# Local attention in six layers: the mask as eight small products, keys transposed before the output product, and three moved steps on VectorE and ScalarE

## What is computed

```python
for i in range(DEPTH):                                   # DEPTH = 6
    x = attn_layer(shift_tokens(x), Wqkv[i], q_scale[i], k_scale[i], Wo[i]) + x
    x = ffn_layer(shift_tokens(x), ...) + x

def attn_layer(x, Wqkv, qs, ksc, Wo):                    # 16 heads of 64
    q, k, v = jnp.split(x @ Wqkv, 3, -1)                 # by head
    q = l2norm(q) * qs; k = l2norm(k) * ksc
    q = q * cos * scale + rotate_half(q) * sin * scale
    k = k * cos * inv + rotate_half(k) * sin * inv
    out = local_attention(q, k, v)                       # windows of 32 queries
    return out @ Wo

# local_attention: a window of 32 queries looks at its own 32 keys and the 32 before
mask = (it < jb) | (it > jb + w) | (jb == -1)
sim = jnp.einsum('bhwie,bhwje->bhwij', bq, bk2) * QK_SCALE
sim = jnp.where(mask, -jnp.finfo(sim.dtype).max, sim)
out = jnp.einsum('bhwij,bhwje->bhwie', softmax(sim), bv2)
```

## Time and profile before

| | |
|---|---|
| median of 3 runs | 5129.18 us (5128.84 to 5138.17) |
| profiled execution, device time | 5126.68 us |
| its span in the trace | 5124.9 us |
| TensorE busy | 4668.2 us, 91% |
| VectorE busy | 3785.3 us, 74% |
| ScalarE busy | 2776.0 us, 54% |
| GpSimd busy | 2074.7 us, 40% |
| granted TensorE clock, mean | 0.968 of 2.4 GHz |

### The profile page before, as it was taken

The page is one execution under the profiler, slowest core; times in us unless marked ns, Lnnn a source line. Parts: engine busy times, 40 slices in busy tenths (PEclk is TensorE's granted clock), DMA queues, the critical chain, the costliest instruction groups (busy, mean ns, idle before and its releaser), DMA issues. The chain is left out here.

```text
span 5124.9 us, 167765 instructions
## 1 busy us (share of the span) xinstructions
PE 4668.2 (91%) x74640; PEld 2826.5 (55%) x74640; DVE 3785.3 (74%) x4462; ACT 2776.0 (54%) x3791; POOL 2074.7 (40%) x1499
## 2 busy tenths in 40 slices
PE   7858987998789869999999999999999999999998
PEld 5623334444333346665666466655666566746664
DVE  5667883333778568886888588868887688868885
ACT  4527774223467645555555455555555455555554
POOL 4330000001000046654666366636665466546661
PEclk9979998999799989999999999999999999999999
DMA  0021111000111121111111111111111111111110
GB/s 23 12 69 32 44 43 34 1 0 27 59 38 43 28 62 40 40 37 45 40 40 40 43 40 40 39 40 40 40 40 52 31 40 40 36 43 40 40 40 26
DMA packets 95777, 192.82 MB, mean 38 GB/s; under 512 B 27088, under 2 KB 45520, under 8 KB 93264
## 3 DMA queue, kind: packets, MB, share of 16 engines
q1 hardware_dynamic: 95056, 182.09, 13.9%
HBM read 60.36 MB, written 15.73 MB: 15 GB/s over the span
## 5 line engine op out<-in xcount | busy, mean ns | idle before, releaser
L1846 POOL TENSOR_TENSOR part_of_layer<-part_of_layer,sine_of_layer 128x512 f32<-128x512 f32 x768 | 963.1, 1275 | 640.0 <-DVE sine_of_layer L1718 640.0
L1853 POOL TENSOR_TENSOR part_of_layer<-part_of_layer,inverse_of_layer 128x1024 f32<-128x1024 f32 x384 | 730.3, 1902 | 325.0 <-ACT inverse_of_layer L1601 310.0
L967 ACT ACTIVATE prob_of_ca<-ps 128x1024 f32<-128x1024 f32 (+3 forms) x768 | 594.0, 814 | 263.5 <-PE ps L841 197.6
L1715 DVE TENSOR_TENSOR part_of_layer<-ps,rope 128x1024 f32<-128x1024 f32 x384 | 467.6, 1218 | 46.8 <-ACT square_of_layer L1589 36.0
L1632 ACT ACTIVATE values_of_layer<-ps 128x1024 f32<-128x1024 f32 x192 | 196.5, 1024 | 516.3 <-PE ps L1488 516.3
L1718 DVE TENSOR_TENSOR sine_of_layer<-ps,rope 128x1024 f32<-128x1024 f32 x384 | 465.1, 1211 | 0.0
L859 PE MATMUL ps<-keys_of_ca,queries_of_ca 64*128 64x512 bf16 (+3 forms) x1536 | 331.1, 342 | 133.7 <-DVE top_of_ca L999 60.9
L1507 PEld LDWEIGHTS ps<-prob_t_of_layer,mixed_of_layer 64*64 64x64 f32 x12288 | 338.0, 134 | 161.0 <-issue 151.7
L1416 PE MATMUL ps<-qkv,shifted 128*128 128x512 f32 x768 | 384.3, 622 | 26.8 <-POOL values_of_layer L1856 20.4
L1758 DVE TENSOR_REDUCE total_of_layer<-prob_of_layer 128x16 f32<-128x1024 f32 x192 | 234.2, 1220 | 229.1 <-ACT prob_of_layer L1625 229.1
L1507 PE MATMUL ps<-prob_t_of_layer,mixed_of_layer 64*64 64x32 f32 x12288 | 385.6, 220 | 10.6 <-ACT prob_t_of_layer L1616 6.7
(11 more groups left out here) (206 smaller groups left out, 9248.5 us busy)
## 6 DMA issues: line engine op xcount, KB each, us to landing
mixed_of_layer<-values_of_layer SPq DMA_DIRECT2D x636, 128.0 KB
mixed_of_layer<-values_of_layer SPq DMA_DIRECT2D x264, 64.0 KB
queries_of_ca<-q_parts SPq DMA_DIRECT2D x384, 32.0 KB
keys_of_ca<-k_parts SPq DMA_DIRECT2D x384, 32.0 KB
qkv<-in_qkv SPq DMA_DIRECT2D x6, 1536.0 KB, 6.5
q_parts<-parts_of_ci SPq DMA_DIRECT2D x16, 384.0 KB, 2.6
k_parts<-parts_of_ci SPq DMA_DIRECT2D x16, 384.0 KB, 2.6
rope<-in_rope SPq DMA_DIRECT2D x6, 1024.0 KB, 9.0
```

Source lines behind the costliest of these rows:

```text
L967: nc.scalar.activation(prob[:, i % 2, 2 * two:2 * two + 2, j:], ps[:, 2 * two:2 * two + 2, j:], ACT.Exp, scale=scale).then_inc(raised, 1)
L1715: nc.vector.tensor_tensor(part[:, t % 2, side], by_head(slot), table(2 * side, t), ALU.mult).then_inc(parts, 1)
L1846: nc.gpsimd.tensor_tensor(out, out, sine[:, side, :, (1 - to) * half:(2 - to) * half], ALU.add).then_inc(rotated, 1)
L1853: nc.gpsimd.tensor_tensor(part[:, t % 2, side], part[:, t % 2, side], by, ALU.mult).then_inc(scaled, 1)
```

## The change

On TensorE the mask is added by eight products of a 32x32 identity with 32 rows of the table (four windows of 32 queries times two halves of the heads) instead of two products of a 128x128 identity with all 128 rows. The table for the first tile of a sequence now masks the look-back in every window's rows, and only window 0 of that tile uses it. `turn_k` stands behind `turn_q`, ahead of `project`. On VectorE `even` stands behind the query rotation of the next step, and `lengths` is cut in two: the keys' sums stand behind `shift`. The lower bound is now a second instruction of each half, and `invert` on ScalarE is cut in two as well, the keys' half behind `raise_p`.

```diff
                 def score(t):
                     reach(pe, l, k_out, t + 1)
-                    for h in range(2):
-                        nc.tensor.matmul(two_banks(SCORE_SLOT)[:, h, :], k["ident_b"][:, :],
-                                         w["band"][:, int(t % TILES == 0), :], start=True, stop=False)
+                    for i in range(P // WIN):
+                        for h in range(2):
+                            rows = slice(h * WIN, (h + 1) * WIN)
+                            nc.tensor.matmul(two_banks(SCORE_SLOT)[i * WIN:(i + 1) * WIN, h, :], k["ident_b"][rows, rows],
+                                             w["band"][rows, int(t % TILES == 0 and i == 0), :], start=True, stop=False)
...
-                    steps((make_next_q, 0), (make_k, 0), (turn_q, 1), (project, 3), (last(lambda: turn(1)), 2), (turn_k, 1),
+                    steps((make_next_q, 0), (make_k, 0), (turn_q, 1), (turn_k, 1), (project, 3), (last(lambda: turn(1)), 2),
                           (turn_p, 2), (score, 1), (last(lambda: turn(0)), 1), (make_v, 0), (weigh, 2),
...
-                def invert(t):
+                def invert(t, side, guarded, logged, inverted):
+                    at = slice(side * HEADS, (side + 1) * HEADS)
                     reach(act, l, guarded, t + 1)
-                    nc.scalar.activation(root[:, t % 2], length[:, t % 2], ACT.Ln).then_inc(logged, 1)
+                    nc.scalar.activation(root[:, t % 2, at], length[:, t % 2, at], ACT.Ln).then_inc(logged, 1)
                     reach(act, l, logged, t + 1)
-                    nc.scalar.activation(inverse[:, t % 2], root[:, t % 2], ACT.Exp, scale=-0.5).then_inc(inverted, 1)
+                    nc.scalar.activation(inverse[:, t % 2, at], root[:, t % 2, at], ACT.Exp, scale=-0.5).then_inc(inverted, 1)
...
-                    steps((square_next_q, 0), (square_k, 0), (out_q, 1), (out_k, 1), (out_p, 2), (last(first_invert), 2), (invert, 0),
-                          (out_v, 0), (raise_p, 1), (last(lambda: square_of(0)), 1), (out_o, 2), (shift_low, 4))
+                    steps((square_next_q, 0), (square_k, 0), (out_q, 1), (out_k, 1), (out_p, 2), (last(first_invert), 2), (invert_q, 0),
+                          (out_v, 0), (raise_p, 1), (last(lambda: square_of(0)), 1), (invert_k, 0), (out_o, 2), (shift_low, 4))
...
-                def lengths(t):
-                    reach(dve, l, q_squared, t + 1)
-                    nc.vector.reduce_sum(length[:, t % 2, 0:HEADS], square[:, 0], AX_X).then_inc(summed, 1)
-                    reach(dve, l, k_squared, t + 1)
-                    nc.vector.reduce_sum(length[:, t % 2, HEADS:], square[:, 1], AX_X).then_inc(summed, 1)
+                def lengths(t, side, squared, guarded):
+                    mine = length[:, t % 2, side * HEADS:(side + 1) * HEADS]
+                    reach(dve, l, squared, t + 1)
+                    nc.vector.reduce_sum(mine, square[:, side], AX_X).then_inc(summed, 1)
+                    reach(dve, l, summed, 2 * t + side + 1)
+                    nc.vector.tensor_scalar(mine, mine, LEAST_SQUARE, None, ALU.max).then_inc(guarded, 1)
...
-                    steps((rotate_q, 0), (lengths, 0), (guard, 0), (rotate_k, 0), (maxima, 1), (shift, 1), (last(first_centre), 1),
-                          (add, 3), (totals, 1), (even, 1), (last(second_centre), 1), (last(third_centre), 2))
+                    steps((rotate_q, 0), (even, 2), (lengths_q, 0), (rotate_k, 0), (maxima, 1), (shift, 1), (last(first_centre), 1), (lengths_k, 0),
+                          (add, 3), (totals, 1), (last(second_centre), 1), (last(third_centre), 2))
...
-    band = np.stack([seen, seen & ((at >= WIN)[:, None] | (key >= 0)[None, :])], 1)
+    band = np.stack([seen, seen & (key >= 0)[None, :]], 1)
```

23 lines of the change are left out of this document (15 added, 8 removed).

## The result

| | median, us | ratio to before, 95% interval |
|---|---|---|
| before | 5132.97 (5128.84 to 5138.17, 4 runs) | |
| changed | 5295.35 (5292.32 to 5307.08, 4 runs) | 1.0325 (1.0313 to 1.0337) |

The change makes the kernel 162 us slower; 5262 had been predicted, with 5200 to 5325 as the range. The profiled execution of the changed kernel took 5307.08 us, with a span of 5305.3.

A forecast was written before the change was run, and what follows sets the result against it. TensorE's own program was taken to bound each step. Per layer 28 x 0.61 = 17.1, plus 2.6, minus 2.1, plus 4.7 = 22.3 us, 134 in six layers, gave 5262 us, range 5200 to 5325.

The forecast's parts named there:

- The wait: Keys' transposes cannot start before 5.57, behind the chain product, squares, two rotation products; TensorE waits 1.16 each step.
- The step: Undisturbed step: 14.17 + 1.16 - 0.41 = 14.92, less 0.14 gained at the mask: 14.78, 0.61 more.
- the best bound: Mask: all eight products at once, 0.32 from mask to scores, gain 0.22 instead of 0.14.
- The poor end of the range: Mask with 0.10 more for the extra tiling switch, head 0, tail +6: 28.5 a layer, 5300.
- The split sums: VectorE, ScalarE: first part hidden; second lower bound ends near 15.25, copy starts 0.99 after the step; `shift_low` costs 2.6 a layer.
- The head: Steps 1 to 3 of a layer: rotation comes earlier with `even` behind it; -2.1 us, between 0 and -3.
- The tail: Layer's end: last `even` behind `second_centre` 3.7 later, output product behind keys' transposes adds 1.0; +4.7, between +3 and +6.
- Mask pieces two or one at a time: Mask's products run two at a time, 5359, chance 0.08; or wholly serial, 5507, chance 0.03.
- ScalarE late in each step: Second lower bound held by GpSimd's addition, ScalarE's copy ends past the squares' place: 101 us more, 5363, chance 0.06.
- Faster, by stretches of TensorE's own that the wait absorbs: Stretches before the new wait absorbed, mask's 0.54 gone too, tail free: 5121; chance 0.03, 0.01 for over 0.2% faster.
- A wrong reading of the code: Keys' transposes would start at 4.41, without waiting for VectorE; given no chance of its own.
- The clock in the steps: New wait drops TensorE's clock, a fifth of steps at 1.2 GHz: about 400 us more, 5662, chance 0.03.

The follow-up runs named there:

- keys_only: The kernel before with only the keys' transposes moved ahead of the output product: 5285.54 us, ratio 1.0305.
- cut2: The kernel before with the keys' transposes placed after two of the output product's eight parts: 5205.86 us, ratio 1.0149.
- cut6: The kernel before with the keys' transposes placed after six of the output product's eight parts: 5090.72 us, ratio 0.9921.
- mask_only: The kernel before with only the mask's eight products and the new table: 5115.12 us, ratio 0.9971.
- last_even_back: The changed kernel with `even` of each layer's last tile put back behind `totals`: 5253.35 us, ratio 1.0242.
- even_only: The kernel before with only `even` moved behind the next step's query rotation: 5190.7 us, ratio 1.0118.
- keys_back: The changed kernel with the keys' transposes put back behind the output product: 5236.1 us, ratio 1.0206.
- after_cut6: The changed kernel with the last tile's `even` put back and the keys' transposes after six of the output product's eight parts: 5206.74 us, ratio 1.0147.
- split_only: The kernel before with only sums, lower bounds and inverse norms split by queries and keys: 5136.13 us, ratio 1.0014.

## Why the prediction was right, and where its terms were off

**The wait: right.** It was put at 5.57 after the step's start; measured 3450.66 - 3445.08 = 5.58. It carries the verdict: keys_only costs 3.05%, and cut2 and cut6 follow the same number. That nothing shortens the chain held against the kernel before, where the rotation starts at 3.08 as it does now. But with the transposes moved and `even` left in its place the rotation would usually have been at 3.29 (keys_only). So the moved `even` keeps some 0.2 a step from being lost, which the prediction did not see: its 14.92 for the step before the mask's gain is 15.15 in keys_only's median.

**The step: 14.78 predicted; measured 14.84 at the shortest, 14.92 in the median.** Most of the difference to the shortest is the mask, taken as 0.40 from mask to scores. It is 0.34 (3454.32 to 3454.66), near the best bound, that of all eight at once. But the time from the probabilities' transposes to the mask grew as well. keys_only has the old mask with no wait before it (timeline):

```profile
2704.11 1.04 PE L1459 MATMUL ps<-sb_ident,prob_of_layer 128*128 128x128 f32 x8
2704.99 0.59 PE L1466 MATMUL ps<-band,sb_ident_b 128*128 128x512 bf16 x2
2705.51 1.49 PE L1475 MATMUL ps<-keys_of_layer,queries_of_layer 64*32 64x64 f32 x128
```

Here 0.88 and 0.52, in the changed kernel 0.97 and 0.34. The gain is 1.40 - 1.31 = 0.09, not 0.14. The extra 0.09 stands just where the array goes from whole to 32x32 pieces. The Trainium skill (TensorEngine Tiling (Array Packing), Key Properties) says that a change of tiling mode drains TensorE. The trace agrees so far as it has 0.09 more in that place. The poor end of the range held 0.10 for it, the sum nothing. In mask_only the 0.09 lies under the wait for ScalarE's copy, so the mask earns the full 0.20 there.

**The split sums: right in their end, wrong in the reading of the first half.** Second lower bound until 15.25: measured 4384.95 + 0.48 - 4370.00 = 15.43. Copy of the weighted values 0.99 after the step: 0.81 (4370.81). `shift_low` pushes by 0.2 (squares at 2.23 instead of 2.03), not 0.43, so 1.2 a layer for 2.6. The first lower bound was to be hidden; it is 1.23 long, since I left out what `even` does to GpSimd. What stood behind the sum, "the new wait absorbs", was true and covered this too. The Trainium skill (SBUF — State Buffer, SBUF: two separate sides) names this case: a VectorE instruction with two inputs in SBUF and a GpSimd instruction that reads SBUF exclude each other for a whole instruction. `even` is such a one and the rotation, whose one input is in PSUM, is not; the trace agrees with 3.42 and 3.35 beside `even`, 2.52 without.

**The head: -2.1 predicted, about -0.7 measured** (38.4 us from step 0 to step 3, before 39.1).

**The tail: +4.7 predicted, +9.5 measured.** This is the term with the largest error, 4.8 x 6 = 29 of the 33 us missing. Its mechanism was right: the last `even` waits behind `second_centre`. Its size was worked out at full clock.

The experiments split it. The order on TensorE alone is worth 2.2 (keys_only, 109.1) and is what is left without the late `even` (last_even_back, 2.0 over before); for it 1.0 had been taken. The late `even` is worth 7.5 (last_even_back) to 7.9 (even_only); for it 3.7 had been taken, its own delay and nothing behind it. The end of the third layer's attention, TensorE in the changed kernel (timeline; before: the earlier trace rows):

```profile
3462.96 1.39 PE L1450 MATMUL ps<-sb_ident,part_of_layer 128*128 128x128 f32 x8 [1.92 <-POOL part_of_layer L1867]
3464.14 3.33 PE L1522 MATMUL ps<-heads_out_of_layer,wo 128*128 128x128 f32 x16
...
3475.56 3.78 PE L1522 MATMUL ps<-heads_out_of_layer,wo 128*128 128x128 f32 x16 [2.19 <-ACT heads_out_of_layer L1632]
...
3483.63 1.57 PE L1461 MATMUL ps<-sb_ident,prob_of_layer 128*128 128x128 f32 x8 [3.43 <-DVE prob_of_layer L1780]
...
3491.09 3.58 PE L1522 MATMUL ps<-heads_out_of_layer,wo 128*128 128x128 f32 x16
```

and the granted clock of the first 40 us of it (busy times by engine, clock, DMA share), with the same stretch of the kernel before in the second fence:

```profile
3459.46:3500.00 40.54, 30.02 (x539) 25.66 (x533) 17.71 (x28) 15.39 (x24) 6.46 (x6) 0.75 0.17 52
```

```profile
3371.26:3408.00 36.74, 30.33 (x528) 23.22 (x522) 21.97 (x33) 18.08 (x27) 7.45 (x7) 0.95 0.30 104
```

The output product, 1.95 at full clock, takes 3.33, 3.78 and 3.58: it runs at 1.2 GHz for most of that time (granted clock 0.56, 0.50 and 0.52). In this layer even the first of them does, and so the mask behind it stands 3.8 later than before, counted from the last step's start (3468.27 - 3445.08 = 23.19, before 3376.57 - 3357.15 = 19.42). In three of the six layers (the first, fourth and fifth) that product is still at full clock, and the mask is about 2 later. The last probabilities are transposed 38.55 after the last step's start instead of 30.85, so `even` adds 3.9 here, near the 3.7 predicted. What the prediction lacked comes behind: from there to the last output product it is 2.1 longer, and that product itself 1.5. Before, only one output product of the three in this layer fell to that clock. The idle times ahead of the slow ones (1.92, 2.19, 3.43 here, 1.35 before) are longer.

The same end in last_even_back (timeline of TensorE) has its last output product at full clock:

```profile
3457.89 2.05 PE L1522 MATMUL ps<-heads_out_of_layer,wo 128*128 128x128 f32 x16 [0.56 <-ACT heads_out_of_layer L1632]
```

So it is in all six layers of last_even_back and in five of before. In the changed kernel and in even_only this product is slow in all six. The lower clock at the end thus comes with the late `even`.

**The rivals.** Mask pieces two or one at a time: no, 0.34. ScalarE late in each step: not in the changed kernel, but it is what keys_back and after_cut6 show, by another route than I wrote. Faster, by stretches of TensorE's own that the wait absorbs: hardly, the time over the shortest step is 29, some 7 of it `shift_low`'s, before 25. A wrong reading of the code: no, the transposes waited. The clock in the steps: no, 1.01 of idle time in 14.85 left it at 1.00 (stretch 3023.74 to 3430.00):

```profile
3023.74:3430.00 406.26, 379.32 (x8641) 264.19 (x8642) 369.50 (x379) 237.00 (x331) 265.01 (x169) 1.00 0.16 38
```

**The sum** by measured terms: 28 x 0.70 (mean steps 15.01 against 14.31, `shift_low` in them) = 19.6 where 19.7 had been predicted, head -0.7, tail +9.5: 28.4 a layer, 170 in six. The two profiled executions differ by 5307.1 - 5126.7 = 180, since that of the changed kernel is the longest of its runs; the medians differ by 162. Of the 10 us between 170 and 180, 6.4 lie ahead of the first layer, in code that the change does not touch (its first queries' product starts at 1833.3, before at 1826.9), and 3 at the last layer's end, which is 12.4 longer and not 9.5 (137.1 against 124.7 from the last step to the end).

That 19.6 meets 19.7 is luck in part. The shortest step is 0.68 longer and not 0.61, 2.0 more a layer; the push by `shift_low` is 1.4 less, and TensorE's own stretches take 0.6 less than before.

## What to carry to other kernels

When a group is moved on the engine that bounds the kernel, work out the earliest time at which what it waits for can be there, and the place it would get; the same move gains up to that point and loses from it on, and a part of the covering work (here six of eight pairs) can be left in front. An edit tested alone says little about a kernel with another edit in it: a long wait on the bounding engine hides what the helpers do, and where it is taken away their own ring comes out. Where a stage drains at its end, price what stands there at the lower clock.

## What the runs showed that was not expected

- Eight bf16 products on 32x32 pieces with 512 columns each take 0.34 from the first to the scores, where two whole ones take 0.52. Ahead of them, where the array goes from whole to 32x32 pieces, stand 0.09 more.
- `even` on VectorE (inputs in SBUF) holds GpSimd's additions by 0.9, and a lower bound on 16 numbers a partition waits up to 1.23 for them.
- The same holds the other way round: where `even` comes while GpSimd's product with the inverse norm is running, it takes 1.70 to 1.98 (medians of keys_only and split_only; 1.33 before).
- TensorE has holes of about 1.1, mostly in the weighting, with no semaphore behind them. All 167 of 0.6 us and more end 1.18 to 1.61 us after a 16 KiB packet of the instruction queue. The time over the shortest step went 25, 42, 82 us for 0, 6 and 14 more instructions a step, and 113 where the last waits were gone as well. Why even_only has holes in 21 steps with no instruction more stays open.
